# Pausing GpSimd's row gathers while TensorE does the table look-ups, and loading the small tables in two transfers

## The reference, cut to what matters

```python
e = jnp.stack([tbl_0[ids[:, 0]], ..., tbl_38[ids[:, 38]]], axis=1)   # 512 samples x 39 features x 16
# two layers of feature products, Xi starts as X0 = e
z = jnp.einsum('bmd,bnd->bdmn', X0, Xi)          # all pairs of features
Xi = jnp.einsum('bdp,po->bod', z.reshape(...), W)  # W0: 1521 -> 128, then W1: 39*128 -> 128
...
h = concat([sum over d of both layers' Xi, dense_ctx])
y = relu(relu(h @ W_top1 + b_top1) @ W_top2 + b_top2) @ W_top3
```

## Time and profile before

| what | us |
|---|---|
| median of 3 runs | 417.27 (416.95 to 417.56) |
| the profiled execution, its own time | 415.95 |
| its span, first to last instruction | 414.1 |
| PE busy, share of the span | 258.1 (62%) |
| DVE, ACT, POOL busy | 187.7, 143.8, 116.3 |

### The profile page before, as it was taken

The page is one execution under the profiler, slowest core; times in us unless marked ns, Lnnn a source line. Parts: engine busy times, 40 slices in busy tenths (PEclk is TensorE's granted clock), DMA queues, the critical chain, the costliest instruction groups (busy, mean ns, idle before and its releaser), DMA issues.

```text
span 414.1 us, 4652 instructions
## 1 busy us (share of the span) xinstructions
PE 258.1 (62%) x1616; PEld 191.0 (46%) x1616; DVE 187.7 (45%) x331; ACT 143.8 (35%) x287; POOL 116.3 (28%) x122
## 2 busy tenths in 40 slices
PE   5501111000000000756999999999999999999998
PEld 5401000000000000652567566777777777788677
DVE  1443110000000000357997399839998398864000
ACT  3221200000000000013574567656776576644411
POOL 5777877777777770000000000000000000000000
PEclk9855555555555555575899799999999999999999
DMA  4890000000000000000431211011000011100000
GB/s 98 223 312 10 6 6 6 7 6 6 7 6 6 7 7 1 2 2 4 107 89 41 59 17 20 15 35 18 14 15 14 10 16 17 16 11 12 12 0 3
DMA packets 35748, 13.07 MB, mean 32 GB/s; under 512 B 21391, under 2 KB 35254, under 8 KB 35724
## 3 DMA queue, kind: packets, MB, share of 16 engines
q1 hardware_dynamic: 30518, 10.92, 11.1%
q0 software_dynamic: 3776, 0.97, 2.4%
q10 hardware_dynamic: 1430, 0.88, 0.7%
HBM read 7.51 MB, written 0.00 MB: 18 GB/s over the span
## 4 chain that ended last, share of the span: by engine, by line
PE 53%; issue 28%; DVE 8%; another core or an unknown queue 6%; ACT 3%; DMA 1%; DVEq 0%; SPq 0%; ACTq 0%
PE s_bank L862 8%; PE b_bank L805 6%; PE l_bank L826 4%; PE l_bank L828 4%; PE l_bank L827 4%; PE b_bank L741 3%; PE l_bank L820 3%; DVE z L639 2%; PE g_bank L848 2%; PE g_bank L849 2%; PE g_bank L850 2%; PE turn_bank L761 2%; PE b_bank L887 2%; PE xi_bank L835 2%
## 5 line engine op out<-in xcount | busy, mean ns | idle before, releaser
L314 POOL DMA_INDIRECT emb<-tbl,ids_sb x118 | 116.1, 984 | 38.9 <-issue 35.7
L639 DVE TENSOR_TENSOR z<-xa,b_bank 128x512 f32<-128x512 f32 (+1 forms) x112 | 76.0, 682 | 33.4 <-ACT xa L395 18.9
L459 ACT ACTIVATE z_hi<-z 128x512 fp32r<-128x512 f32 (+1 forms) x96 | 60.5, 630 | 24.6 <-DVE z L639 23.6
L559 DVE TENSOR_SCALAR xa<-g,numbers 125x1024 bf16<-125x1024 int16 x16 | 7.8, 524 | 124.1 <-remote 113.6
L653 DVE TENSOR_TENSOR z_lo<-z,z_hi 128x512 fp32r<-128x512 f32 x80 | 54.6, 684 | 0.0
L741 PE MATMUL b_bank<-g,w_sb 125*128 125x48 bf16 x77 | 8.2, 208 | 72.8 <-issue 72.8
L805 PE MATMUL b_bank<-xs,sel 117*128 117x512 bf16 (+1 forms) x112 | 45.4, 407 | 5.7 <-DVE z L639 4.6
L375 ACT ACTIVATE parts<-emb 128x304 bf16<-128x304 f32 (+6 forms) x12 | 4.4, 366 | 125.7 <-DVE emb L575 125.7
L741 PE MATMUL b_bank<-g,xa 125*128 125x48 bf16 x64 | 9.0, 206 | 62.6 <-issue 51.1
L862 PE MATMUL s_bank<-g,w_sb 128*128 128x128 f32 x312 | 46.2, 277 | 0.0
L862 PEld LDWEIGHTS s_bank<-g,w_sb 128*128 128x128 f32 x312 | 41.8, 191 | 1.9 <-issue 1.3
(11 more groups left out here) (114 smaller groups left out, 374.4 us busy)
## 6 DMA issues: line engine op xcount, KB each, us to landing
diag<-z SPq DMA_DIRECT2D x1, 2560.0 KB
diag<-xt SPq DMA_DIRECT2D x128, 20.0 KB, 1.9
w_sb<-w SPq DMA_DIRECT2D x3, 832.0 KB, 5.2
emb<-tbl,ids_sb POOLq DMA_INDIRECT x118
wt_sb<-wt SPq DMA_DIRECT2D x2, 512.0 KB
g<-tbl ACTq DMA_DIRECT2D x11, 78.1 KB
g<-tbl SPq DMA_DIRECT2D x8, 62.5 KB
w0p<-w_pair SPq DMA_DIRECT2D x1, 448.0 KB
```

The lines of the kernel that those rows point to most:

```text
L314: nc.gpsimd.indirect_dma_start(emb[:, bt, n * D:(n + 1) * D], None, tables[order[n]], bass.IndirectOffsetOnAxis(ids_sb[:, bt, order[n]:ord ...
L459: nc.scalar.activation(z_hi[0:rows, s % RING, :], z[0:rows, at, :], ACT.Copy).then_inc(rounded, 1)
L639: nc.vector.tensor_tensor(target, xa[0:rows, bt % 2, c * CB:(c + 1) * CB, :].rearrange("p b d -> p (b d)"), b_bank[s % B_RING][0:rows, :], ...
```

## The change: what it does

1. POOL gathers tile 0's 20 large features as before, then waits until `looked_up` has reached 36 (both tiles' look-ups are through), and then gathers the other 98.
2. The host lays the small tables of each class side by side, partition by partition. SP loads each class in one transfer (4,096 and 7,040 bytes for a partition) in place of 8 on SP and 11 on ACT. ACT issues no transfers any more.
3. ACT's `table_cast(1, 1)` (the second part of the 1,250-row class) stands ahead of the last two of tile 1's id copies, not behind them.

```diff
@@ gpsimd
             for bt in range(TILES):
+                if bt == 1:
+                    pool.wait_ge(looked_up, LOOK_TILES * MATCHES)
                 for k, (lo, hi) in enumerate(groups[bt]):
@@ sync
-            lo, hi = classes[0]
-            for n in range(lo, hi):
-                sp.dma_start(table[0][:, n - lo, :, :],
-                             tables[order[n]].rearrange("(p c) d -> p c d", p=LOOK_P)).then_inc(table_in[0], 16)
+            for k in range(len(classes)):
+                sp.dma_start(table[k].rearrange("p n c d -> p (n c d)"), small_tables[k]).then_inc(table_in[k], 16)
@@ scalar
-            def load_tables(lo, hi):
-                for n in range(lo, hi):
-                    act.dma_start(table[1][:, n - classes[1][0], :, :],
-                                  tables[order[n]].rearrange("(p c) d -> p c d", p=LOOK_P)).then_inc(table_in[1], 16)
-
             def table_cast(part, k):
                 if part == 0:
-                    act.wait_ge(table_in[k], 16 * (classes[k][1] - classes[k][0]))
+                    act.wait_ge(table_in[k], 16)
...
-            lo, hi = classes[1]
-            load_tables(lo, lo + EARLY)
             act.wait_ge(ids_in, 16)
             nc.scalar.activation(ids_f, ids_sb[:, 0:LOOK_TILES, :], ACT.Copy).then_inc(ids_cast, 1)
-            load_tables(lo + EARLY, hi)
             take_ids(0, 0, len(ids_groups))
             table_cast(0, 0)
             take_ids(1, 0, 2)
             table_cast(1, 0)
             table_cast(0, 1)
-            take_ids(1, 2, len(ids_groups))
+            take_ids(1, 2, 3)
             table_cast(1, 1)
+            take_ids(1, 3, len(ids_groups))
@@ host
+    for k, c in enumerate(blocks):
+        arrays[f"small_{k}"] = np.concatenate([a[f"tbl_{f}"].reshape(LOOK_P, c * D) for f in order
+                                               if rows[f] == LOOK_P * c], axis=1)
```

More of the change, by code:

```diff
@@ L60 @@
 LOOK_SPLIT = 9
-EARLY = 5
 IDS_GROUP = 4
@@ L103, in chunk_at, with build @@
     return i if rest == 0 and 0 <= i < CHUNKS else None
-def build(nc, ids, row_numbers, tables, order, dense_t, w0_pair, w0_mirror, w1,
+def build(nc, ids, row_numbers, small_tables, tables, order, dense_t, w0_pair, w0_mirror, w1,
           wt1, bt1, wt2, bt2, wt3, select, ident16, ident32, out):
@@ L1050 @@
     tables = [aps.pop(f"tbl_{f}") for f in range(F)]
+    small_tables = [aps.pop(f"small_{k}") for k in range(len(blocks))]
     out = nc.dram_tensor("y", (B, 1), mybir.dt.float32, kind="ExternalOutput").ap()
-    build(nc, tables=tables, order=order, out=out, **aps)
+    build(nc, tables=tables, small_tables=small_tables, order=order, out=out, **aps)
     return run_bass_kernel_spmd(nc, [arrays], core_ids=[0]).results[0]["y"]
```

## The result

The changed kernel takes **386.12 us** (386.06 to 386.68, 4 runs) beside 417.41 (416.95 to 417.58, 4 runs) for the kernel before: a ratio of **0.9255**, 95% interval 0.9239 to 0.9271, 7.5% faster. The prediction was 409; the time lies in its stated range (285 to 421), but outside its likeliest case's own, 395 to 416. PE's crawl did move into the main phase, but the end comes 23 us earlier than forecast.

A forecast was written before the change was run, and what follows sets the result against it. Bound by look-ups in which PE crawls while POOL gathers, then a PE-bound main phase. Gathers landed 175.5, tail 12.9, main phase 230.6 less 13: span 406.0, on the medians' scale 409 us; range 285 to 421.

The forecast's parts named there:

- likeliest case: Main phase beside the moved gathers: PE crawls there too; 395 to 416 us, chance 0.42.
- PE crawls while POOL gathers: Start of the kernel before: PE sinks to 2.8 us a look-up during gathers, comes back some 13 us after.
- I take the crawl: Main phase beside the 98 moved gathers: PE is slowed as in the look-ups, for 120 us.
- B: Main phase runs at full speed beside the gathers: time 289, range 285 to 305 us; chance 0.30.
- D: Look-ups: the crawl has nothing to do with the gathers; time as before, 416 to 418 us; chance 0.06.
- E: Main phase: slower, by the late end of the gathers; up to span 420, time 423 us; chance 0.10.
- C: Main phase: mild crawl, a third to half of its pace kept; 360 to 385 us; chance 0.12.
- I take 13: Main-phase work done under the crawl, beside the moved gathers: 13 us, taken off its 230.6.
- with the undisturbed first 4 us: Main phase's beginning beside the gathers: 4 us unslowed, making 18 us of work done, counted by instructions, into 22.
- the bounds of 8 and 18: Main-phase work done under the crawl: some 8 us counted by share of time, 18 us counted by instructions.
- `looked_up` is full at ... 52: End of both tiles' look-ups with the pause: 35 + 3 + 14 = 52 us in place of 179.5.
- Two transfers for 19 ... The crawl's releases hide it: 0: Table loading at the start: merged transfers bring 0, or 1.8 us if the releases did not hide it.

The follow-up runs named there:

- run 3: Changed kernel with the 98 gathers of tiles 1 to 3 left out, SP loading wrong rows in 8 plain transfers, on a crawling chip: 276.34 us.
- 7: Changed kernel on a crawling chip, three runs: 98 indirect gathers of rows 0 to 127, 385.51 us; memsets without those gathers, 279.04; gathers 2.23 us apart, 364.48.
- the pause alone: Kernel before with only POOL's wait added, tables in 19 transfers and the old order of ACT's casts, on a crawling chip: 392.9 us, ratio 0.9418.
- run 4: Changed kernel with each of the 98 gathers replaced by a plain transfer of 128 rows of 64 bytes from POOL, on a crawling chip: 277.13 us.

## Why the prediction was right and wrong

**Right: the mechanism.** "PE crawls while POOL gathers" and "I take the crawl" hold (runs 3 and 7). The trace shows what was named: the pause, look-ups at speed in it, PE at four tenths or less from 67 us until 165, DVE waiting for PE. B, D and E fell on this chip. C didn't hold either: it wanted 40 to 60 us of the main phase done by 175, and 26 were. That the time, 386.12, is 1 us above C's range and 9 below the likeliest case's comes from the two terms below.

**Wrong: two terms of the sum.** The sum said 406.0 for the span; 384.3 was measured. Term by term: `looked_up` full at 41.7 and not 52, -10.3; POOL's 98 gathers 123.8 us and not 122.5, +1.3; from POOL's end to PE's return 14.5 and not 13.9, +0.6; main-phase work done by then 26.4 us (230.6 less the 204.2 that were left at 180.1) and not 13, -13.4. Together -21.8.

*"I take 13" is the larger miss,* and the pause alone shows it by itself: there `looked_up` is full at 53.9, 1.9 us behind the forecast, and still the time is 392.9 and not 409. The step that failed is "with the undisturbed first 4 us". The forecast took the onset from the start of the kernel before, where PE slows 5.7 us after the first gather. After the restart PE kept its pace for 18 us, so some 14 us of the main phase (45.5 to 59.8) were done at once; the other 12 us, in the crawl and its tail, lie between the bounds of 8 and 18 for it. What sets the onset stays open. In the changed kernel and in the pause alone it falls at the same step, 14.0 us after the first turn, and just then SP's small `diag` transfers begin; time beside gathers and these transfers were not told apart. The early onset in the kernel before fell together with the loading of tables and weights; that the loading deepened it is only argued.

*"`looked_up` is full at ... 52"* was near for the pause alone: 53.9, with the first look-up at 34.3 and not 38. The step that failed is "Two transfers for 19 ... The crawl's releases hide it: 0". With the moved cast, also put at nothing, the transfers brought 12.2 us. I had read only who waits for a table, ACT once for 1.8 us. But with the transfers merged the id turns come out of PE sooner, 11.51 in place of 13.69, 18.79 in place of 26.41, 28.51 in place of 45.49, and PE is already at speed at 29.7, with one gather to come. The start was limited by PE's pace in the crawl, and that is what changed. Whether the fewer packets, the earlier start of the casts or the wider gaps between gathers while other transfers are under way do it was not separated. (The bounds "46 to 61" are off too: by the terms beside them they are 49 and 62.)

**What the prediction could not see.** That the crawl belongs to some chips. On a quiet chip B's mechanism holds: with the look-ups' end at 36.9 us in place of 52 its 289 becomes 274, and 272.55 was measured. The row that I used against it, the crawl with only PE and POOL at work, was true of crawling chips alone.

**The rule against it.** "DMA never contends with a compute engine" ("SBUF — State Buffer", "Who interferes with whom", the Trainium skill) holds in the plain transfers: 98 of them from POOL cost PE nothing (run 4). For indirect ones on a crawling chip the runs show 110 us, and the measurement decides.

## What to carry to other kernels

When one engine is slow with no wait of its own, ask what else was going on in just that stretch, and test it by leaving that out, as run 3 did. A pause that protects a short stage only moves the interference, and pays by what overlaps before it sets in; moving the gathers took 417 to 386, lowering their rate as well took it to 313, and the lower rate costs 24 us or more on a chip that doesn't need it. And run the kernel before on the chip of the experiment: 281 and 417 us were the same program.

## What the runs showed of the hardware

- PE sinks to some 2.2 to 2.8 us a matmul beside indirect gathers that POOL issues every 1.25 us, on two of the four chips of the experiments. It does so neither beside plain transfers of the same size from POOL every 0.53 us, nor beside memsets on POOL; indirect gathers of contiguous rows do it as well (385.51 us).
- It sets in 6 to 18 us after the gathers start. Once deep it lasts 14 us after they end; in its shallow beginning PE was back at speed within 5 us of the last gather (29.3 to 34.3, the pause alone). At one gather every 1.66 us or slower it is nearly gone; near one in 1.44 us times scatter from 300 to 321 us.
- What in the chip links the two engines stays open, and so does what tells the chips apart.
